# Indirect stores of a group begun in the iteration of its places, the last group's score subtractions on VectorE, and the padding zeroed an iteration sooner

## The reference

```python
x = x + attn(cond(x, itok_B_0_7, w1), wq, wk, wv, wp)
x = x + ffn(cond2(x, itok_B_1_198, w2), router_w, gate_w, up_w, down_w)
# cond:  out[b,d,t] = sum_c x[b,c,t] * w[index[b],c,d]       (32x32 weights of each sequence)
# attn:  16 heads of 16; every projection is subln -> 8-bit rounding -> ternary weights;
#        scores / 4, causal mask, softmax over the 32 tokens, times v, then wp
# ffn:   softmax router over 16 experts, the best 2, weights renormalised;
#        expert e: (silu(x @ gate[e]) * (x @ up[e])) @ down[e], 256 -> 96 -> 256
```

## Time and profile before

| what | value |
|---|---|
| median of 3 runs | 461.99 us (460.49 to 463.59) |
| the profiled execution | 461.3 us |
| its span in the trace | 459.6 us, 10906 instructions |
| mean granted TensorE clock | 0.895 of full speed |
| chain that ended last, by engine | PE 46%, DVE 18%, issue 12%, DMA 8%, ACT 5% |

### The profile page before, as it was taken

One profiled execution on the slowest core, in us unless ns is written; L12 is line 12 of the kernel. 1 busy time (PEld: TensorE's weight loads), 2 busy tenths in 40 slices (PEclk: granted clock), 3 DMA queues, 4 the chain that ended last, 5 costly groups with the idle time before them and its releaser, 6 DMA issues.

```text
span 459.6 us, 10906 instructions
## 1 busy us (share of the span) xinstructions
PE 337.1 (73%) x3258; PEld 248.0 (54%) x3273; DVE 258.9 (56%) x876; ACT 244.7 (53%) x580; POOL 219.9 (48%) x262
## 2 busy tenths in 40 slices
PE   5777989999899989887755039898788879884000
PEld 1433647676766666555644028776667667672000
DVE  2535677999798979847544443333333333331665
ACT  9163888888687887837444015444544544442000
POOL 7162242346566473827477713565455545554000
PEclk9799999999999999979857559999999999998555
DMA  5617555445554546256675554454454445420999
GB/s 183 199 53 150 122 131 112 91 109 141 155 130 113 121 110 135 74 142 153 167 202 154 220 168 118 138 152 133 134 146 120 137 137 149 129 67 2 355 398 343
DMA packets 76897, 68.87 MB, mean 150 GB/s; under 512 B 41002, under 2 KB 65967, under 8 KB 76720
## 3 DMA queue, kind: packets, MB, share of 16 engines
q1 hardware_dynamic: 65008, 43.76, 37.4%
q0 software_dynamic: 7296, 20.02, 12.0%
q10 hardware_dynamic: 4544, 4.46, 2.9%
HBM read 35.36 MB, written 30.62 MB: 144 GB/s over the span
## 4 chain that ended last, share of the span: by engine, by line
PE 46%; DVE 18%; issue 12%; DMA 8%; ACT 5%; SPq 4%; DVEq 3%; another core or an unknown queue 2%; POOL 1%; ACTq 1%; POOLq 0%
PE bank L1386 12%; PE bank L1397 7%; DMA arena<-y_d 3%; SPq L414 3%; PE bank L1379 3%; PE bank L1249 3%; PE bank L1132 2%; PE bank L1234 2%; PE bank L1221 2%; PE bank L1392 2%; PE bank L1155 2%; PE bank L1170 2%; PE bank L1285 2%; PE bank L1298 2%
## 5 line engine op out<-in xcount | busy, mean ns | idle before, releaser
L559 POOL DMA_INDIRECT y_d<-cen,di x79 | 77.8, 985 | 78.2 <-ACT cen L770 54.9
L1078 DVE SCALAR_TENSOR_TENSOR kT<-kT,hrow,bank 128x96 f32<-128x96 f32 x79 | 24.8, 314 | 96.4 <-ACT kT L765 77.6
L513 POOL DMA_INDIRECT routed<-hrow,posi x64 | 65.2, 1019 | 16.5 <-issue 16.5
L1386 PE MATMUL bank<-arena,qT 128*128 x316 | 66.9, 335 | 4.2 <-ACT qT L760 3.5
L494 POOL TENSOR_TENSOR sc<-sc,mx 128x512 f32<-128x512 f32 x32 | 33.7, 1052 | 53.7 <-DVE mx L889 53.4
L1386 PEld LDWEIGHTS bank<-arena,qT 128*128 128x128 f32 x316 | 50.8, 194 | 6.5 <-issue 6.5
L1397 PE MATMUL bank<-arena,sc 96*128 x158 | 49.3, 394 | 1.5 <-DVE sc L1085 1.4
L770 ACT ACTIVATE cen<-bank 128x256 f32<-128x256 f32 x79 | 30.5, 386 | 33.3 <-PE bank L1397 22.8
L1379 PE MATMUL bank<-ident,hrow 128*128 128x128 f32 x158 | 31.1, 280 | 21.8 <-issue 21.8
L760 ACT ACTIVATE qT<-bank 128x256 f32<-128x256 f32 x79 | 30.2, 383 | 24.4 <-PE bank L1379 23.8
L765 ACT ACTIVATE kT<-bank 128x96 f32<-128x96 f32 x79 | 20.0, 253 | 41.3 <-PE bank L1386 36.4
(11 more groups left out here) (173 smaller groups left out, 713.1 us busy)
## 6 DMA issues: line engine op xcount, KB each, us to landing
hrow<-routed SPq DMA_DIRECT2D x79, 129.0 KB
arena<-y_d SPq DMA_DIRECT2D x16, 512.0 KB, 12.4
v_d<-v_sb SPq DMA_DIRECT2D x8, 544.0 KB
vx<-v_d SPq DMA_DIRECT2D x32, 136.0 KB
X<-in_x SPq DMA_DIRECT2D x8, 512.0 KB, 3.8
out_x<-X ACTq DMA_DIRECT2D x16, 256.0 KB, 8.2
arena<-kT SPq DMA_DIRECT2D x60, 64.0 KB
arena<-in_L_ffn_gate_w SPq DMA_DIRECT2D x4, 384.0 KB
```

Source lines behind the costliest of these rows:

```text
L513: g_.indirect_dma_start(routed, bass.IndirectOffsetOnAxis(ap=posi[g % 2][:, t, k:k + 1], axis=0), hrow[:, g % 2, t, k, :], None).then_inc( ...
L559: g_.indirect_dma_start(y_d, bass.IndirectOffsetOnAxis(ap=di[:, n:n + 1], axis=0), ye[n], None, bounds_check=Y_ROWS - 1, oob_is_err=False) ...
L1386: last = t_.matmul(bank[2 + n][:, 0:2 * F], xeT[n][:, c, :], gu[:, c, bass.ds(expert(k - 1), 1), :].rearrange("p o f -> p (o f)"), start=( ...
```

## The change

It has four parts.

- The stores of group g: five of them, (0,0), (0,1), (1,0), (1,1) and (2,0), are issued in iteration g + 3, that of the places: two behind sub_max 2 and three behind sub_max 3. The other three follow in iteration g + 4: (2,1) behind rstd_x, (3,0) behind number, (3,1) behind sub_max 1.
- POOL's sub_max leaves out the last group. VectorE has a new step sub_last, straight behind each row_max, which does this subtraction for the last group alone, in iteration 8, behind a drain.
- zero_pad moves from the end of iteration 9 to iteration 8, ahead of the first five stores of group 5.
- put_pad moves from iteration 11 to iteration 10, between the stores (2,0) and (2,1) of group 7.

```diff
@@ -488,7 +488,7 @@
                 g_.tensor_tensor(rstd[:, 1, :], veps[:, 1, :], half[:, 1, :], ALU.pow).then_inc(o_rstd_ok, 1)
 
             def sub_max(g, t):
-                if absent(g):
+                if not 0 <= g < GROUPS - 1:
                     return
                 wait(pool, mx_ok, g, TG, t + 1)
                 g_.tensor_tensor(sc[t % 2][:, :, :], sc[t % 2][:, :, :], mx[t % 2][:, :].unsqueeze(2).to_broadcast([P, H, SEQ]),
@@ -524,27 +524,27 @@
                 g_.indirect_dma_start(routed, bass.IndirectOffsetOnAxis(ap=pad_i[:, 0:1], axis=0), pad.rearrange("p k r -> p (k r)"), None).then_inc(padded, 16)
 
             def iteration(it):
-                scatter(it - 4, 0, 0)
                 rstd_x(it)
-                scatter(it - 4, 0, 1)
+                scatter(it - 4, 2, 1)
                 if it == 0:
                     zero_kx1()
                 sub_max(it - 1, 0)
                 rstd_o(it - 2)
                 number(it - 3)
-                scatter(it - 4, 1, 0)
+                scatter(it - 4, 3, 0)
                 sub_max(it - 1, 1)
-                scatter(it - 4, 1, 1)
-                if it == GROUPS + STAGES - 1:
+                scatter(it - 4, 3, 1)
+                sub_max(it - 1, 2)
+                if it == GROUPS:
+                    zero_pad()
+                scatter(it - 3, 0, 0)
+                scatter(it - 3, 0, 1)
+                sub_max(it - 1, 3)
+                scatter(it - 3, 1, 0)
+                scatter(it - 3, 1, 1)
+                scatter(it - 3, 2, 0)
+                if it == GROUPS + STAGES - 2:
                     put_pad()
-                scatter(it - 4, 2, 0)
-                sub_max(it - 1, 2)
-                scatter(it - 4, 2, 1)
-                scatter(it - 4, 3, 0)
-                sub_max(it - 1, 3)
-                scatter(it - 4, 3, 1)
-                if it == GROUPS + 1:
-                    zero_pad()
 
             for it in range(GROUPS + STAGES):
                 iteration(it)
@@ -888,6 +888,14 @@
                     wait(dve, sub_ok, g, TG, TG + t - 1, lag=1)
                 v.tensor_reduce(mx[t % 2][:, :], sc[t % 2][:, :, :], AX.X, ALU.max).then_inc(mx_ok, 1)
 
+            def sub_last(g, t):
+
+                if g != GROUPS - 1:
+                    return
+                dve.drain()
+                v.tensor_tensor(sc[t % 2][:, :, :], sc[t % 2][:, :, :], mx[t % 2][:, :].unsqueeze(2).to_broadcast([P, H, SEQ]),
+                                ALU.subtract).then_inc(sub_ok, 1)
+
             def norm_o(g, t):
                 if absent(g):
                     return
@@ -995,19 +1003,23 @@
                 step_x(it)
                 round_x(it)
                 row_max(it - 1, 0)
+                sub_last(it - 1, 0)
                 rivals(it - 3)
                 route(it - 3)
                 largest_o(it - 2)
                 row_max(it - 1, 1)
+                sub_last(it - 1, 1)
                 factor_o(it - 2)
                 scale_k(it, 0)
                 choose(it - 3)
                 place(it - 3)
                 row_max(it - 1, 2)
+                sub_last(it - 1, 2)
                 scale_k(it, 1)
                 step_o(it - 2)
                 norm_o(it - 1, 0)
                 row_max(it - 1, 3)
+                sub_last(it - 1, 3)
                 residual(it - 2, 0)
                 norm_o(it - 1, 1)
```

## The result

The changed kernel takes 469.69 us (median of four runs, of which one, 475.34 us, ran in a slower state at a lower granted clock; the ratio rests on the other three, 466.91 to 470.07), the kernel before 462.69 on the same chip. The ratio is 1.0138, 95% interval 1.0073 to 1.0204: slower by 1.4%. The profiled execution took 466.91 us with a span of 465.1, against 461.3 and 459.6 before, at the same mean clock (0.898 against 0.895). So 5.5 us of span are to be found. The prediction was 462.4, range 459.0 to 465.0.

The account below looks back on a forecast made before the run. No engine was above 73% busy, so the kernel was taken as a row of stages waiting in turn. Terms 0 + 1.0 + 0 - 0.3 - 0.3 = +0.4 us on 461.3 gave 461.7, as a median 462.4; range 459.0 to 465.0.

Parts of the forecast that it names:

- Step 1: Stores reordered in the steady iterations: 0 us per iteration, over five iterations -1.0 to +1.0.
- a sign of being wrong: In the steady iterations: an iteration pitch off from 24.7 us by over 0.3 us.
- Step 2: Iteration 8, four subtractions on VectorE at 0.69 us plus a drain: +1.0 us, bounds 0 to +3.1.
- rival B: Iteration 8: VectorE becomes its bound, all four subtractions in series on the chain; +2.8 us, 464.8 us; chance 0.18.
- Step 3: Clearing of the padding moved to iteration 8, where POOL has nothing due: cost 0, up to 1 us if TensorE were faster.
- Step 4: End of the stores: POOL ends 1.6 us sooner, hidden; VectorE's table keeps its 6.1 us of waits; -0.3 and -0.3.
- Rival A: VectorE's table comes free of POOL and loses 3 instead of 6.1 us: -2.9, 459.1 us; chance 0.17.
- rival C: The stores gate the expert stage, VectorE's table doesn't, so the last slot's 1.6 us count: -0.9, 461.1 us; chance 0.15.

Follow-up runs that it names:

- e1: The kernel before with only the new order of the stores and the padding's store; subtractions stay on POOL, clearing in iteration 9: ratio 1.0125.
- e4: The changed kernel with the padding's store behind two of group 7's stores instead of five, and the clearing ahead of group 5's: ratio 1.0232 to the kernel before.
- h1: The changed kernel with group 5's stores put behind iteration 9's root instead of behind the clearing: ratio 1.0201 to the kernel before.
- e3: The kernel before with its stores reordered so that none stands between subtraction 3 and the next iteration's root; subtractions stay on POOL: ratio 1.0006.
- g1: Against the kernel before: two stores ahead of subtraction 3, none behind; last group's subtractions on VectorE; clearing early in iteration 8; padding two stores behind the last places: 1.016.
- e2: The kernel before with only the last group's four subtractions moved to VectorE, stores in the old order: ratio 1.0117.
- f3: e3's steady order with the last group's subtractions on VectorE, iteration 8 ending with the clearing and no store, padding behind two group 7 stores: 1.0086 to the kernel before.
- f4: As f3, but five stores of group 5 follow the clearing in iteration 8 and a sixth heads iteration 9: ratio 1.0094 to the kernel before.
- f1: The kernel before with 64 small matmuls more on TensorE ahead of the first iteration: ratio 1.0019.
- f2: The kernel before with 64 drains put ahead of VectorE's program: ratio 0.9976.
- g2: e3 with three plain 128x256 writes to a spare tensor, issued by POOL behind subtraction 3 of iterations 3 to 7: ratio 1.0012 to the kernel before.

## Why the prediction was wrong

- **Step 1, the stores in the steady iterations: failed.** It said "Cost 0", since POOL had 1.7 us spare before its root. POOL did have them: the train of 98.12 ends at 101.65 and the root waits for its moments. But the stores were not looked at from the other engines. The four kernels with three stores behind subtraction 3 (after, e1, e4, h1) need 100.6 to 102.9 us for the four pitches; the kernels with the order of before 97.0 to 98.7, those with the order of e3 95.7 to 97.7. The term was -1.0 to +1.0 and measured +4.5 (after), +3.3 (e1), a pitch of 25.4 instead of 24.3 us, which the prediction itself had named as a sign of being wrong. Which of the stores does it is only half shown: the waits of 3 us stand at turns with three, but g1, with two of them ahead of subtraction 3 and none behind it, has no excess wait there and takes 99.0 us, 1.9 over e3 and hardly more than e2's 98.7; and no run took a single store from such a turn.
- **Step 2, the subtractions on VectorE: right in the durations, too high in the sum.** Each took 0.69 us, as the earlier trace rows gave; e1 and after, which differ in them and in the clearing, are alike within 0.6 us from iteration 7 to the last places, and in e2 iteration 8 to 9 is 0.1 us longer than before, not 1.0. The bound of +3.1 and rival B fall. The open question of a two-operand subtraction beside the clearing or a store is settled: the one at 219.33 lies within the clearing of 217.72 and takes 0.69, the one at 222.03 beside two stores takes 0.69, and L871 inside the clearing takes 0.21 instead of 0.64. By the rule of the Trainium skill, page "SBUF — State Buffer", section "Who interferes with whom", a GpSimd instruction that only writes doesn't contend: the trace agrees, with 0.69 us inside the clearing.
- **Step 3, the clearing moved: failed, in the part "Cost 0; if TensorE were faster there, up to 1 us".** POOL's times were as forecast: the clearing started 5.6 us behind iteration 8's rivals (217.72; the estimate of 214 to 214.8 is 5.7 to 6.5 behind those of the kernel before), the six stores ended 16.6 behind them (228.70; the forecast 226.1 is 17.8), and the root behind them was not late. What the step didn't see is that VectorE and ScalarE get TensorE's results only about when the train ends: +3.0 us net from iteration 8 to 9, 6.7 by f3 against f4, and 6.4 from iteration 7 to 9 by h1 against after.
- **Step 4, the end: POOL as forecast, VectorE not.** POOL waited 5.4 us for the places (4 forecast) and ended at +12.10 (12.6 forecast). "I keep all of it" for the table's 6.1 us was wrong: they all went. Rival A named it with half the size. But its gain of time was wrong as well, since rival C's gate stood behind it: with the table free the last store, landing late behind the padding of +7.00, set the first load, at +16.45. That this is again 16.4 us behind the places is coincidence: something else ends the wait. The step's sentence that "the stores' landing was at most as late as the register load" was true of before by 0.02 us, and there lay the limit on any gain.
- **The range** had its upper end from bounds on POOL's and VectorE's own time. None of the rivals priced what a longer train does to third engines, though the kernel before shows it: 3.20 us at 225.41 with three stores against 1.47 with none, and the "remote" wait of 2.15 us in the earlier trace rows, which I had read as cover for VectorE.
- **Slips that change nothing.** The stores' pitch is 0.96 + 0.30 = 1.26 us in the steady iterations, and 1.28 only at the end; 24.7 us is one pitch, the mean of four is 24.3; the sums of rivals B and C take only one of the forecast's two terms of -0.3.

No version beat the kernel before. e3_clear equals it within its interval, as do f1, f2 and g2. The parts that each gain in a profiled execution (a turn free of stores, 2 us in f3 against e2; the padding issued early, 2.4 us in g1) were never had together: in f3 and h1 the stores kept away from a turn were still to be issued later.

## What to carry to other kernels

Before indirect stores are moved into an engine's idle time, look at what the other engines wait for during the whole train, above all at results of a third engine: one or two stores in a row at a turn mostly cost nothing here, three mostly added 1.5 us of wait, and six up to 6. A wait that the profile puts to nobody beside such a train belongs to it until shown otherwise, and isn't slack. And where a stage starts when several things are done, work out when each of them would let it start; here two lay 0.02 us apart and the 6 us taken from one gave nothing.

## What the runs showed of the hardware

- A result of TensorE, recorded as finished at 223.04, was signalled at 230.03 and taken up by ScalarE at 230.05. At eight trains of three to nine indirect stores a result came 0.9 to 1.6 us behind the train's end; the exceptions are named above. Three plain DMAs from POOL or ScalarE left the wait at 1.47.
- VectorE's small instructions met waits of about 0.3 to 1.8 us without a releaser, 5 to 6 us in all, when POOL had issued seven or eight stores without a pause of 2 us beforehand, 1.45 us after six, and none after four or fewer (a correlation over fourteen kernels).
- POOL's indirect store takes 0.97 us, but up to 2.27 beside a 128x1264 VectorE instruction with both inputs in SBUF.
- A store of 2.1 MB landed 7.0 to 7.4 us behind its issue. A store of 128 rows issued 4.1 us behind it landed 5.0 to 5.1 us after its own issue, one issued 7.7 to 9.3 us behind it 2.5 to 2.8.
